# Second layer with four buffers, first batch norm by halves, and fp32 rows in an LSTM stage's output

## The reference

```python
A_norm = adj + eye(128);  A_hat = A_norm * dinv[:, None] * dinv[None, :]
y = relu(batchnorm((A_hat @ x) @ W1.T + b1, g1, be1))      # 256 channels
z = batchnorm(y @ W2.T + b2, g2, be2)                      # 128 channels
x1 = layernorm(x + z)                                      # per node
h = relu(adj @ (x1 @ Wg0 + bg0)); h = relu(adj @ (h @ Wg1 + bg1))
for p in (1, 2, 3, 4):
    # every run of p nodes (time steps) is fed to an LSTM of 128 units, whose last
    # hidden state replaces h at the run's last step
    h[:, p-1::p] = lstm_last(Wih[p-1], Whh[p-1], b[p-1], windows(h, p))
out = layernorm(x1 + h)
```

## Time and profile before

| what | us |
|---|---|
| median of 3 runs (783.59 to 784.75) | 784.45 |
| the profiled execution, its own time | 785.71 |
| its span, first to last instruction | 783.90 |
| PE busy / DVE busy / ACT busy / POOL busy | 741.4 / 673.0 / 531.8 / 318.9 |
| PE's share of the chain that ended last | 70% |
| DVE's share of it | 18% |
| mean granted TensorE clock | 0.972 of full |

### The profile page before, as it was taken

How to read it: one execution, slowest core, us unless ns; L and a number is a source line. 1 busy time by engine, 2 the same in 40 slices (tenths; PEclk the granted TensorE clock), 3 DMA queues, 4 the chain that set the end, 5 groups by cost and what they waited for, 6 DMA issues and landing times.

```text
span 783.9 us, 11543 instructions
## 1 busy us (share of the span) xinstructions
PE 741.4 (95%) x3922; PEld 417.8 (53%) x3922; DVE 673.0 (86%) x1419; ACT 531.8 (68%) x856; POOL 318.9 (41%) x282
## 2 busy tenths in 40 slices
PE   6999699878999999998999999999999999999993
PEld 4777333357677777764444444444454545555441
DVE  5888677777998989965888787999999998989998
ACT  3788578635677687656888686877666768657551
POOL 1000000048787887850000000053469684394792
PEclk9999799969999999999999999999999999999996
DMA  7433400012323233210700000001011103210013
GB/s 213 124 110 107 108 0 0 0 28 81 90 74 108 80 83 108 68 41 1 322 1 1 1 0 1 1 0 41 1 41 41 41 1 107 68 41 28 1 41 94
DMA packets 62987, 45.03 MB, mean 57 GB/s; under 512 B 1578, under 2 KB 61396, under 8 KB 61908
## 3 DMA queue, kind: packets, MB, share of 16 engines
q1 hardware_dynamic: 62932, 44.33, 18.7%
HBM read 27.55 MB, written 16.78 MB: 57 GB/s over the span
## 4 chain that ended last, share of the span: by engine, by line
PE 70%; DVE 18%; ACT 6%; issue 3%; DMA 1%; SPq 1%; POOL 0%; DVEq 0%
PE ps L616 10%; PE ps L625 10%; PE ps L617 10%; PE ps L592 8%; PE ps L630 6%; PE ps L622 6%; PE ps L621 6%; ACT work L812 4%; PE ps L540 3%; DVE ln_stats L1042 3%; DVE ring L1024 2%; DVE ring L1060 2%; DVE store L1071 2%; PE ps L552 2%; PE ps L551 2%
## 5 line engine op out<-in xcount | busy, mean ns | idle before, releaser
L812 ACT ACTIVATE work<-ps,gate_bias 128x512 f32<-128x512 f32 (+1 forms) x449 | 280.6, 680 | 82.2 <-PE ps L630 46.8
L616 PE MATMUL ps<-store,wih 128*128 128x512 f16 (+1 forms) x449 | 169.6, 378 | 3.3 <-issue 2.3
L617 PE MATMUL ps<-store,wih 128*128 128x512 f16 (+1 forms) x449 | 169.5, 378 | 0.0
L625 PE MATMUL ps<-store,wih 128*128 128x512 f16 (+1 forms) x449 | 158.7, 378 | 0.0
L509 POOL TENSOR_TENSOR end_mv<-end_mv,minus_half 128x12 f32<-128x12 f32 (+1 forms) x16 | 30.8, 1925 | 265.8 <-DVE end_mv L1036 265.8
L500 POOL TENSOR_SCALAR ring<-ring,ln_mv 128x128 f32<-128x128 f32 x120 | 120.4, 1015 | 2.6 <-POOL ln_mv L490 2.5
L1007 DVE TENSOR_TENSOR work<-work 128x512 f32<-128x512 f32 (+1 forms) x129 | 88.4, 685 | 20.4 <-ACT work L819 20.4
L819 ACT ACTIVATE work<-store 128x512 f32<-128x512 f32 (+1 forms) x97 | 60.4, 623 | 66.5 <-DVE store L1000 51.5
L621 PE MATMUL ps<-store,whh 128*128 128x512 f16 (+1 forms) x248 | 93.2, 376 | 0.0
L622 PE MATMUL ps<-store,whh 128*128 128x512 f16 (+1 forms) x248 | 93.1, 376 | 0.0
L630 PE MATMUL ps<-store,whh 128*128 128x512 f16 (+1 forms) x248 | 93.0, 376 | 0.1
(11 more groups left out here) (121 smaller groups left out, 1251.1 us busy)
## 6 DMA issues: line engine op xcount, KB each, us to landing
ring<-in_x_dram SPq DMA_DIRECT2D x32, 256.0 KB, 2.8
ring<-in_x_dram SPq DMA_DIRECT2D x16, 512.0 KB, 5.3
x_scratch<-ring SPq DMA_DIRECT2D x16, 512.0 KB, 3.5
ring<-x_scratch SPq DMA_DIRECT2D x5, 1024.0 KB, 4.8
out_dram<-ring SPq DMA_DIRECT2D x5, 768.0 KB, 3.5
store<-x_scratch SPq DMA_DIRECT2D x3, 1024.0 KB, 13.3
out_dram<-store SPq DMA_DIRECT2D x3, 768.0 KB, 3.5
out_dram<-ring SPq DMA_DIRECT2D x5, 256.0 KB, 2.3
```

Of the source, the lines that this page charges most:

```text
L616: nc.tensor.matmul(acc(j), w_hi, x_hi, start=True, stop=False)
L617: nc.tensor.matmul(acc(j), w_lo, x_hi, start=False, stop=False)
L625: last = nc.tensor.matmul(acc(j), weights(wih, j)[0], x_lo, start=False, stop=u.first)
L812: nc.scalar.activation(acts[:, n % 2, gate, 0:u.cols], ps[:, gate_bank(q), 0:u.cols], ACT.Tanh if gate == G else ACT.Sigmoid, bias=gate_bi ...
```

## The change

*Second layer.* The loop is written out; `relu1` gets four buffers (two more in `work`), the result four banks. PE waits for each relu half by itself. DVE takes `bn_stats` straight from PSUM, without b2, then stores with b2 added; for the last chunk `bn_aggr` comes ahead of the store, and b2 is added to the mean in a step of its own. *Batch norm* goes column by column: two for the first, one for the second. *LSTM stage.* The eight units 4.tile.3 are `kept`: their hidden state stays in fp32 in `acts`, has no high or low part, and is turned from there by four fp32 transposes, in the place right behind the next unit; waits that counted units count units with parts (`halves_through`), and ACT's gates two units later wait for the turn. `LATE` has another order of the same units; the last eight are 4.4.3 4.5.2 4.7.1 4.6.2 4.5.3 4.7.2 4.6.3 4.7.3 (numbers 121 to 128), the kept units are 95, 107, 114, 113, 121, 125, 127, 128 for tiles 0 to 7. `TAIL` is row 3 of tiles 6 and 7; tile 6's add goes ahead of the last unit's hidden state.

```diff
+    def kept(self):
+        return self.p == 4 and self.last
...
 LATE = """
-    2.0.0 2.1.0 2.2.0 2.0.1 2.1.1 2.4.0 2.2.1 2.3.0 2.4.1 3.0.0
...
-    3.8.2 4.3.3 3.10.2 4.4.1 4.5.1 4.7.0 4.6.0 4.4.2 4.5.2 4.6.1
-    4.7.1 4.4.3 4.5.3 4.7.2 4.6.2 4.7.3 4.6.3
+    2.1.0 2.2.0 2.0.0 2.1.1 2.2.1 2.4.0 2.5.0 2.0.1 3.1.0 2.4.1
+    2.3.0 3.0.0 2.5.1 2.7.0 3.1.1 2.8.0 2.3.1 2.8.1 2.6.0 3.2.0
+    2.7.1 2.6.1 3.0.1 3.1.2 2.10.0 2.9.0 3.0.2 3.3.0 3.4.0 4.0.0
...
+    4.3.1 4.1.2 3.9.0 3.10.0 4.3.2 4.1.3 3.9.1 3.10.1 4.5.0 3.9.2
+    3.8.2 4.3.3 4.2.3 3.10.2 4.6.0 4.4.2 4.5.1 4.6.1 4.7.0 4.4.3
+    4.5.2 4.7.1 4.6.2 4.5.3 4.7.2 4.6.3 4.7.3
...
+HALVES0 = [sum(not u.kept for u in UNITS[:n]) for n in range(len(UNITS) + 1)]
+def halves_through(n):
+    return HALVES0[n + 1]
...
+    fixed = {}
+    for tile in range(P // T_TILE):
+        fixed[NUMBER[Unit(4, tile, 3)] + 1] = tile
...
-        wanted.append((NUMBER[Unit(4, tile, 3)] + 2, tile, range(3, 4)))
+    places, free = [(at, (tile, 3)) for at, tile in fixed.items()], 0
...
-TAIL = [piece for n in sorted(MOMENTS) if n >= len(UNITS) - 1 - TAIL_UNITS for piece in MOMENTS[n]]
+TAIL = MOMENTS[len(UNITS) - 1]
...
+        relu1 = [ring[:, k, :].rearrange("p (h n) -> p h n", h=H1) for k in (4, 5)] + \
+            [work[:, k:k + H1, :] for k in (0, H1)]
+        RELUS = OUTS = 4
...
+            def second_layer(c):
+                wait(pe, out_stored, c + 1 - OUTS)
                 for h in range(H1):
-                    last = nc.tensor.matmul(ps[:, q % 2, :], w2T[:, h, :], relu1[:, q % 2, h, :],
+                    pe.wait_ge(relu_done, H1 * c + h + 1)
+                    last = nc.tensor.matmul(ps[:, c % OUTS, :], w2T[:, h, :], relu1[c % RELUS][:, h, :],
                                             start=(h == 0), stop=(h == H1 - 1))
...
             def turn_h(tile, r):
                 if r == 3:
-                    pe.wait_ge(lo_done, NUMBER[Unit(4, tile, 3)] + 1)
+                    pe.wait_ge(hid_done, last + 1)
...
+                    if r == 3:
+                        done = nc.tensor.transpose(acc, acts[:, last % 2, O, m * P:(m + 1) * P], ident[:])
+                        continue
...
+            def relu_chunk(c):
+                wait(act, out_summed, c + 1 - RELUS)
                 for h in range(H1):
+                    if c == 0:
+                        act.wait_ge(bn_ready, h + 1)
...
-                        wait(act, lo_done, n - 1)
+                        before = UNITS[n - 2]
+                        if before.kept:
+                            act.wait_ge(h_turned, TURN_ORDER.index((before.tile, 3)) + 1)
+                        else:
+                            act.wait_ge(lo_done, halves_through(n - 2))
...
-            batch_norm(0, H1, 2, VG1, VBE1, 0)
+            for h in range(H1):
+                batch_norm(h, VG1 + h, VBE1 + h)
...
+                nc.vector.bn_stats(st2[:, c, :], ps[:, c % OUTS, :]).then_inc(out_stats, 1)
...
+            for c in range(CHUNKS):
+                out_statistics(c)
+                if c == CHUNKS - 1:
+                    dve.wait_ge(out_stats, CHUNKS)
+                    nc.vector.bn_aggr(mean_var[:, H1, :], st2[:].rearrange("p c s -> p (c s)")).then_inc(bn_moments, 1)
+                store_out(c)
+            dve.wait_ge(bn_moments, H1 + 1)
+            nc.vector.tensor_tensor(mean_var[:, H1, 0:1], mean_var[:, H1, 0:1], vec[:, VB2:VB2 + 1], ALU.add)\
+                .then_inc(out_mean, 1)
...
-                if delayed:
+                if delayed and not UNITS[n - 1].kept:
                     hidden_lo(n - 1)
...
+                else:
+                    for tile, r in ADDS[end][:-1]:
+                        end_add(tile, r)
                 hidden(n)
-                hidden_hi(n)
+                if not UNITS[n].kept:
+                    hidden_hi(n)
```

More of the change, by code:

```diff
@@ L152, in ln_slots @@
         ready = max(NUMBER[v] for v in sources(Unit(4, tile, 0))) + 2
-        wanted.append((max(ready, NUMBER[Unit(4, tile, 0)]), tile, range(0, 3)))
-        wanted.append((NUMBER[Unit(4, tile, 3)] + 2, tile, range(3, 4)))
[L155 to L162, removed]
+        wanted.append((max(ready, NUMBER[Unit(4, tile, 0)]), tile))
+    places, free = [(at, (tile, 3)) for at, tile in fixed.items()], 0
+    for at, tile in sorted(wanted):
+        for r in range(3):
+            at = max(at, free)
+            while at in fixed:
+                at += 1
+            places.append((at, (tile, r)))
+            free = at + 1
+    for at, piece in sorted(places):
+        put(turns, at, piece)
+        put(adds, at + 1, piece)
+        if piece[1] >= 2:
+            put(moments, at + 1, (piece[0], 0 if piece[1] == 2 else 3))
     return turns, adds, moments
@@ L476, in _ @@
                 .then_inc(dinv_done, 1)
[L478 to L481, removed]
+            for k in range(H1 + 1):
+                rstd = bn_rstd[:, k:k + 1]
+                pool.wait_ge(bn_moments, k + 1)
+                nc.gpsimd.tensor_scalar(rstd, mean_var[:, k, 1:2], EPS, 1.0, ALU.add, ALU.mult)\
                     .then_inc(bn_rstd_done, 1)
-                pool.wait_ge(bn_rstd_done, 2 * n + 1)
-                nc.gpsimd.tensor_tensor(bn_rstd[:, cols], bn_rstd[:, cols], minus_half[:, 0:width], ALU.pow)\
-                    .then_inc(bn_rstd_done, 1)
+                pool.wait_ge(bn_rstd_done, 2 * k + 1)
+                nc.gpsimd.tensor_tensor(rstd, rstd, minus_half[:, 0:1], ALU.pow).then_inc(bn_rstd_done, 1)
             for n, (g, b0, b1) in enumerate(LN_PIECES):
@@ L716, in turn_h @@
                 n = TURN_ORDER.index((tile, r))
+                last = NUMBER[Unit(4, tile, 3)]
                 if r == 3:
-                    pe.wait_ge(lo_done, NUMBER[Unit(4, tile, 3)] + 1)
+                    pe.wait_ge(hid_done, last + 1)
                 else:
-                    pe.wait_ge(lo_done, max(NUMBER[v] for v in sources(Unit(4, tile, 0))) + 1)
+                    pe.wait_ge(lo_done, halves_through(max(NUMBER[v] for v in sources(Unit(4, tile, 0)))))
                 wait(pe, end_added, n - 1)
@@ L724, in turn_h @@
                     acc = ps[:, TURN + n % 2, m * P:(m + 1) * P]
+                    if r == 3:
+                        done = nc.tensor.transpose(acc, acts[:, last % 2, O, m * P:(m + 1) * P], ident[:])
+                        continue
                     nc.tensor.matmul(acc, hist[:, 0, t, :], ident16[:], start=True, stop=False)
-                    last = nc.tensor.matmul(acc, hist[:, 1, t, :], ident16[:], start=False, stop=True)
-                last.then_inc(h_turned, 1)
+                    done = nc.tensor.matmul(acc, hist[:, 1, t, :], ident16[:], start=False, stop=True)
+                done.then_inc(h_turned, 1)
             pe.wait_ge(w_lo_done, W_JOBS)
@@ L785, in _ @@
                     weights_hi(W_JOB_AT.index(c))
-            act.wait_ge(bn_ready, 1)
-            def relu_chunk(c, q):
-                wait(act, out_summed, c - 1)
+            def relu_chunk(c):
+                wait(act, out_summed, c + 1 - RELUS)
                 for h in range(H1):
-                    nc.scalar.activation(relu1[:, q % 2, h, :], store[:, h, bass.ds(c * BANK, BANK)], ACT.Relu,
+                    if c == 0:
+                        act.wait_ge(bn_ready, h + 1)
+                    nc.scalar.activation(relu1[c % RELUS][:, h, :], store[:, h, c * BANK:(c + 1) * BANK], ACT.Relu,
                                          bias=bn_shift[:, h:h + 1], scale=bn_scale[:, h:h + 1])\
                         .then_inc(relu_done, 1)
-            chunks_by_four(act, relu_chunk)
-            act.wait_ge(bn_ready, 2)
+            for c in range(CHUNKS):
+                relu_chunk(c)
+            act.wait_ge(bn_ready, H1 + 1)
             def gates(n, js=range(4)):
@@ L1169, in _ @@
                         end_moments(piece)
-            for n in range(end - 1, end + 1):
-                for piece in MOMENTS.get(n, ()):
-                    end_scale(piece)
+            for piece in TAIL:
+                end_scale(piece)
 DEG_STEP = 9
```

72 lines of the change are left out of this document (27 added, 45 removed), and 11 rows, old and new, of the table LATE.

## The result

| us | before | changed |
|---|---|---|
| median of 4 runs (lowest to highest) | 784.36 (783.59 to 784.75) | 771.95 (771.08 to 773.20) |
| ratio of the two, 95% interval | | 0.9844 (0.9827 to 0.9861) |
| the profiled execution, its own time / span | 785.71 / 783.9 | 771.08 / 769.3 |
| mean granted clock in it | 0.972 | 0.982 |

The change takes off 12.4 us; 773.7 was forecast, 10.8 less than before. (A fourth run of the kernel before puts its median at 784.36.) The profiled execution of the changed kernel is the fastest of its four, so the two profiles lie 14.6 us apart, 2.2 more than the medians.

What follows compares the result with a forecast made beforehand. PE's own rate bounds the LSTM stage, DVE the tail, with PE waits in the second layer and two batch norm gaps; -1.8 - 4.8 - 0.8 + 1.0 - 4.4 = -10.8 from 784.45 gives 773.7 us, range 769.5 to 779.0.

Steps and rivals of the forecast that it cites:

- First batch norm: Gap before the second layer: working by halves starts PE at 90.75 instead of 92.54, saving 1.8 us.
- Second layer: Four relu buffers and four banks remove PE's waits for ACT and DVE: 62.0 to 57.2, saving 4.8 us.
- The bound set up for ACT: Second layer: two relus take ACT 1.53 us against PE's 1.71 a chunk, so PE bounds next.
- Rival A: Second layer: DVE, ACT or PE's own semaphores become the bound; the 4.8 are not saved, 778.5 us; chance 0.14.
- Statistics from PSUM: Second layer: DVE's statistics read from PSUM were taken at 0.69 us a chunk, within 0.64 to 0.75.
- Second batch norm: Gap after the second layer: last store and its wait leave the chain, saving 0.8 us.
- Cost of the fp32 turns: LSTM stage: four fp32 transposes take 0.435 us against 0.44 for eight fp16 matmuls, so no change.
- Rival B: LSTM stage: each fp32 transpose costs its own 0.273 us between fp16 matmuls, 3.9 more, 777.6 us; chance 0.08.
- Order: LSTM stage: new unit order puts turns closer to hidden states, +1.0 us, between -1.8 and +5.
- Rival C: LSTM stage: hidden states come late for the turns, 14.8 us lost, 787.5 us, slower than before; chance 0.05.
- D: Rival: no pinch and old stalls gone in the LSTM stage, 1.5 us from a kind clock, 769.4 us; chance 0.10.
- Tail: End of the kernel: shorter DVE chain brings its last scaling from 781.12 to 776.7, saving 4.4 us.

Runs made afterwards that it cites:

- e5: Changed kernel with two relu buffers instead of four, four output banks kept: 771.97 us, ratio 0.9838.
- e6: Changed kernel with two output banks instead of four, four relu buffers kept: 770.75 us, ratio 0.9824.
- e9: Changed kernel with two relu buffers and two output banks, still waiting for each relu half by itself: 772.15 us, ratio 0.9835.
- e1: Kernel before with only the second layer and both batch norms of the change: 776.59 us, ratio 0.9908.
- e8: Changed kernel with first batch norm for both halves at once, PE waiting for relu pairs, DVE storing before statistics of the stored chunk: 773.78 us, ratio 0.9865.
- e12: Kernel before with one edit, PE waiting for each relu half by itself in the second layer: 779.81 us, ratio 0.9939.
- e7: Changed kernel with each fp32 transpose of kept rows done three times over: 776.86 us, ratio 0.9906.
- e4: Changed kernel with the old order of LSTM units put back: 778.97 us, ratio 0.9939.
- e11: Changed kernel with matmuls whose results nobody reads added in PE's idle gaps: 767.50 us, ratio 0.9783.

## Why the forecast held, step by step

The single profiles differ in where the clock fell. For the terms I take the median over the profiles of all kernels that have a stage in its old form (3 or 4 of them) or its new one (7 to 9; for the layer with the half wait, e5, e6 and e9 among them):

| us | forecast | old form | new form | measured |
|---|---|---|---|---|
| start of the second layer | -1.8 | 92.2 | 90.6 | -1.6 |
| second layer | -4.8 | 62.0 | 56.9 | -5.1 |
| second gap | -0.8 | 4.33 | 3.37 | -1.0 |
| LSTM stage | +1.0 | 407.8 | 407.1 | -0.7 |
| tail | -4.4 | 15.8 | 12.1 | -3.7 |
| sum | -10.8 | | | -12.1 |

The sum is near the medians' -12.4. It leaves out the graph stage, which the change doesn't touch and for which the forecast had no term: its median is 201.3 us over the four profiles with the old layer and 198.8 over those with the new one. Those 2.5 us would bring the sum to -14.6, and e1's medians leave no room for them, so the agreement is good to some 2 us only. Point by point:

- **First batch norm: right** in size and way; e8 takes it back and starts 1.6 us later. From the first aggregate on, free of what came before, it is 5.17 against 3.44 us, or 1.73.
- **Second layer: right size, but one of two causes overlooked.** That with four of each buffer and bank the waits go is true (e8, where PE still waits for pairs), but the changed kernel doesn't need them: e9 has two of each and the full gain, and e12 gets it from the moved wait alone. The step that failed is the credit for the 4.8 us. The wait for each half, which the prediction used only for the layer's first pass, is enough by itself, so buffers and banks add nothing beside it. The bound set up for ACT, 1.53 against 1.71, compares throughputs; with two buffers what counts is the round of one buffer, and the pair's wait makes PE 0.16 us late for it. The releaser column of the weight loads seemed to say "relu late, 14.2 us", with 4.4 more for DVE's stores; by the spacing of chunks (1.86 against 1.72) the kernel before lost about 4.5 us, the rest was cover under the running matmul. And luck has a share in the size: the forecast left the slow clock as it was, but the layer has 3.4 us at 1.2 GHz in most profiles of the new form and 5.2 to 6.1 in the old, which is some 0.9 of the 5.1. Rival A needed PE, ACT or DVE to take over as the bound: no kernel with the half wait shows it.
- **Statistics from PSUM: right** (0.69 taken, 0.699 measured), and without effect on the layer's length (e8).
- **Second batch norm: right**, 0.2 better.
- **Cost of the fp32 turns: right.** Zero was taken from 0.109 us a transpose; e7 finds 0.109 in place. Rival B, each at its own 0.273, would have put 7.9 us more on e7's stage beyond the 5.2 it shows. The same run answers the Trainium skill ("TensorE: Matmul & The Clock Gate", Part 4: PE-mode transpose): its 275 ns is here the length of one transpose, not the distance to the next, and the granted clock stayed up behind twelve in a row.
- **Order: wrong sign, small.** +1.0 was put on pinches, 0.2 us on each of five places. The changed kernel has none: no turn waits in the LSTM stage. What is left are stalls in the first seven units, as before; the kernel before had three small ones behind them (0.45 us in sum, by the spacing of its matmuls), and these are gone. What I counted as distance to the hidden state was too pessimistic; that the 6.1 us less of DVE work in the stage are the reason is likely, but not shown. Rival C's mechanism exists, though: e4 has it, with waits of up to 2.8 us and 4.8 in all, only under the other order. Of D the missing pinches came true. The clock was kind to the profiled execution in the LSTM stage (406.02 against 407.1) and unkind in the second layer (58.17 against 56.9), so it is not why that one was the fastest.
- **Tail: 0.7 less than forecast.** The mis-sized step is "the cell ends at about 769.2", that is 1.1 us behind the last matmul's end; in the changed kernel it is 1.55 (758.69 against 757.14), since tile 5's add, statistics and moments stand ahead of unit 127's hidden state, and that ahead of the last cell. The other is POOL's root for tile 7: DVE's last scaling waited 0.21 us for it, where the forecast had it ready.

What stays open: why the clock falls for 3.4 us in one execution and 13.7 in another behind the same gap (the second one, in e4 and in the changed kernel). The graph stage ran from 198.5 to 201.5 us over kernels that are identical in it, with 6.8 to 17.1 us at 1.2 GHz, and this scatter of some 3 us is larger than half the terms above. A filler for the stretch that is left in e11 wasn't tried.

## What to carry to other kernels

With a ring of n buffers, compare the round trip (release, refill, signal) with the time until the consumer's next turn for that buffer; if it is late by a tenth of a us or two, a wait for the first part of a refill is as good as another buffer, and costs no memory. Idle time of a weight load with a releaser beside it is no loss as long as matmuls overlap it (18.6 us of it stood for some 4.5 lost): count matmuls in equal stretches, or spacing of starts, instead. Two edits that each lose alone (an order, a shorter path with a tighter place) can pay together, so test them alone and together before one is dropped.

## What the runs showed of the hardware

- Falls to 1.2 GHz came behind or within idle of PE (2.78 us up to 600.69 in e4; 5.30 us up to 90.72 in the changed kernel), and unread matmuls in such gaps kept 2.4 GHz except from 154.5 to 157.9 and gave back 4.4 us (771.95 to 767.50), more than most of the change's own terms. The Trainium skill ("TensorE: Matmul & The Clock Gate", Part 1: The HAM clock gate) says that the engine is throttled unless its activity releases it; these rows agree.
- Twelve fp32 transposes of 128 x 128 ran at 0.109 us each among fp16 matmuls.
- `bn_stats` of 512 fp32 columns cost the same from PSUM (0.699 us) as from SBUF (0.694 us).
- A root of one column on POOL took 0.55 to 0.57 us in all three places by its timeline, though the chain of waits shows a piece of 0.31 for one of them: a piece of the chain is not always an instruction's whole length.
